# Masked attention scores kept in their PSUM bank, a later wait for the values, and a new split of the last head's blocks

## The reference

```python
x = x + tanh(g_xattn) * xattn(layernorm(x), ids, ctx, ctx, ctx)     # 4 experts: silu(h Wg) * (h Wu), then Wd
x = x + tanh(g_ffn)   * ffn(layernorm(x), ...)

# ffn, 16 heads of 32
q, k, v = rmsnorm(x) @ Wq.T, ... @ Wk.T, ... @ Wv.T
probs   = softmax(where(causal, q k^T / sqrt(32), min), -1)
attn    = (probs @ v) @ Wo.T
mod     = 0.1 * tanh(attn @ A)                                      # A: 512 x 16
h       = rmsnorm(residual, ln2)
gate    = silu(h @ W_in.T + mod * (h @ A) @ B)
out     = residual + (gate * (h @ W_up.T)) @ W_down.T               # hidden width 2048
```

## Time and profile before

| | us |
|---|---|
| median of 3 runs (lowest, highest) | 1045.88 (1045.06, 1047.07) |
| profiled execution, whole | 1046.06 |
| its span, first to last instruction | 1044.3 |
| PE / DVE / ACT / POOL busy | 1011.3 / 701.9 / 608.0 / 284.6 |

### The profile page before, as it was taken

The page is one execution under the profiler, slowest core; times in us unless marked ns, Lnnn a source line. Parts: engine busy times, 40 slices in busy tenths (PEclk is TensorE's granted clock), DMA queues, the critical chain, the costliest instruction groups (busy, mean ns, idle before and its releaser), DMA issues.

```text
span 1044.3 us, 16780 instructions
## 1 busy us (share of the span) xinstructions
PE 1011.3 (97%) x5140; PEld 831.4 (80%) x5141; DVE 701.9 (67%) x1837; ACT 608.0 (58%) x1447; POOL 284.6 (27%) x280
## 2 busy tenths in 40 slices
PE   6999999999999999999999999999999989999998
PEld 6787888777888887778888888778888877788887
DVE  7766755996665558985665479966655599854443
ACT  4464456997344448985444369963444489844432
POOL 4536124861000117650000148610001177400000
PEclk9999999999999999999999999999999999999999
DMA  6545133343222426443322354432334253322221
GB/s 236 195 151 171 40 121 96 77 119 132 94 90 90 131 62 169 97 133 115 104 91 91 111 157 92 117 122 91 92 102 147 64 149 92 91 81 90 90 90 51
DMA packets 47073, 115.78 MB, mean 111 GB/s; under 512 B 6800, under 2 KB 6800, under 8 KB 46096
## 3 DMA queue, kind: packets, MB, share of 16 engines
q1 hardware_dynamic: 43968, 105.06, 33.7%
q0 software_dynamic: 3040, 9.96, 2.8%
HBM read 76.46 MB, written 13.37 MB: 86 GB/s over the span
## 4 chain that ended last, share of the span: by engine, by line
PE 86%; DVE 11%; issue 1%; DMA 1%; POOL 1%; ACT 1%; SPq 0%; DVEq 0%; POOLq 0%
PE bank L534 68%; PE bank L731 7%; DVE big L1399 5%; PE bank L793 4%; DVE wr L1385 3%; PE bank L697 2%; PE bank L835 1%; PE bank L590 1%; PE bank L764 1%; PE bank L605 1%; PE bank L648 1%; DMA stack<-wr 0%; PE bank L570 0%; POOL wr L502 0%; DVE big L1422 0%
## 5 line engine op out<-in xcount | busy, mean ns | idle before, releaser
L534 PE MATMUL bank<-hT,wr 128*128 128x512 f32 x1488 | 358.2, 390 | 0.0
L534 PEld LDWEIGHTS bank<-hT,wr 128*128 128x128 f32 x1488 | 279.2, 188 | 60.8 <-issue 1.5
L534 PE MATMUL bank<-wr,actr 128*128 128x512 f32 (+1 forms) x1224 | 303.4, 397 | 2.2 <-DVE actr L1367 1.5
L534 PEld LDWEIGHTS bank<-wr,actr 128*128 128x128 f32 x1224 | 228.9, 190 | 50.8 <-issue 3.0
L490 POOL TENSOR_SCALAR big<-big,rr 128x256 f32<-128x256 f32 (+1 forms) x128 | 154.5, 1215 | 82.4 <-DVE rr L1405 82.4
L429 POOL TENSOR_TENSOR wqs<-wstage,wqs 128x512 fp32r<-128x512 f32 x32 | 43.1, 1358 | 433.6 <-ACT wqs L949 432.2
L1432 DVE SCALAR_TENSOR_TENSOR wr<-stream,lns,wr 128x256 fp32r<-128x256 f32 x256 | 121.7, 537 | 52.2 <-ACT wr L1059 52.2
L1033 ACT ACTIVATE big<-big,nb 128x512 f32<-128x512 f32 (+3 forms) x256 | 140.9, 557 | 11.5 <-DVE nb L1399 11.1
L1385 DVE TENSOR_TENSOR wr<-bank,wr 128x512 fp32r<-128x512 f32 (+1 forms) x224 | 126.0, 607 | 21.3 <-ACT wr L949 20.7
L949 ACT ACTIVATE wr<-bank 128x512 fp32r<-128x512 f32 (+1 forms) x224 | 110.1, 529 | 35.7 <-PE bank L534 20.2
L949 ACT ACTIVATE actr<-act_sb 128x512 fp32r<-128x512 f32 x64 | 40.4, 632 | 146.0 <-DVE act_sb L1446 146.0
(11 more groups left out here) (174 smaller groups left out, 988.0 us busy)
## 6 DMA issues: line engine op xcount, KB each, us to landing
stream<-in_wmlp SPq DMA_DIRECT2D x64, 512.0 KB, 4.0
stack<-wr SPq DMA_DIRECT2D x192, 128.0 KB, 2.3
stream<-in_wmlp SPq DMA_DIRECT2D x64, 256.0 KB, 2.7
big<-in_x SPq DMA_DIRECT2D x4, 1024.0 KB
big<-y_rows SPq DMA_DIRECT2D x4, 1024.0 KB, 5.8
residual<-big SPq DMA_DIRECT2D x4, 1024.0 KB
big<-residual SPq DMA_DIRECT2D x4, 1024.0 KB, 6.5
out<-big SPq DMA_DIRECT2D x3, 1024.0 KB, 4.8
```

Of the source, the lines that this page charges most:

```text
L534: mm = pe.matmul(dst, lhs(pl, k), rhs(pr, k), start=start and i == 0, stop=stop and i == n - 1, skip_group_check=skip)
```

## The change

- `maxima` writes the masked scores back into the bank that it reads (in place), no longer to `prob`. Its wait for `p_turned` is gone, and so is the wait for `res_out` ahead of the first head.
- `exponentials` reads the bank and writes `prob`. Blocks 2 and 0 share a bank, so the exponential of block 2 waits for the maxima of both.
- PE may write new scores into a bank only when the exponentials have read it: every such wait is now on `exp_ok` in place of `nb_ok`, with the same counts.
- The wait for `vst_lo` goes from ahead of the transposes to ahead of the first attend. The DVE copy to `vp` goes from `head_step` of head 0 to ahead of it.
- In the last head DVE scales blocks 3 and 2, POOL block 1 alone. The low-rank product runs whole (8 matmuls) in step 14; step 13 has no filling.

```diff
-NORM_DVE, NORM_ACT, NORM_POOL = 3, 0, (1, 2)
+NORM_DVE, NORM_ACT, NORM_POOL = (3,), 0, (1, 2)
+LAST_DVE, LAST_POOL = (3, 2), (1,)
...
 POOL normalise(n):
-                for qt in NORM_POOL:
+                for qt in NORM_POOL if n % H < H - 1 else LAST_POOL:
...
 PE scores_last(n, ...):
-                    pe.wait_ge(nb_ok, n * 4 - 3)
+                    pe.wait_ge(exp_ok, n * 4 - 3)
 PE scores_middle(n, ...):
-                    pe.wait_ge(nb_ok, n * 4 - 1)
+                    pe.wait_ge(exp_ok, n * 4 - 1)
 PE scores_second(n, ...):
-                    pe.wait_ge(nb_ok, n * 4)
+                    pe.wait_ge(exp_ok, n * 4)
...
 PE filling:
-                elif head >= LOW_RANK_FROM:
-                    low_rank_part(b, head - LOW_RANK_FROM)
+                elif head == LOW_RANK_AT:
+                    low_rank(b)
...
 PE head_step:
-                if j == 0:
-                    pe.wait_ge(vst_lo, b * NQ + q + 1)
                 if head < H - 1:
                     wait_probs(n + 1)
...
                 if head < H - 3:
-                    pe.wait_ge(nb_ok, (n + 3) * 4 - 1)
+                    pe.wait_ge(exp_ok, (n + 3) * 4 - 1)
...
+                    if j == 0:
+                        pe.wait_ge(vst_lo, b * NQ + q + 1)
                     attend(first, HI)
                     if head < H - 3:
-                        pe.wait_ge(nb_ok, (n + 3) * 4)
+                        pe.wait_ge(exp_ok, (n + 3) * 4)
...
 ACT exponentials(n, par):
-                for i, qt in enumerate((3, 2, 0, 1)):
-                    act.wait_ge(nb_ok, n * 4 + i + 1)
-                    rows = prob_rows(par, qt)
-                    a.activation(rows, rows, ACT.Exp, ...
+                for qt, maxima in ((3, 1), (2, 3), (0, 3), (1, 4)):
+                    act.wait_ge(nb_ok, n * 4 + maxima)
+                    bk, col, _ = SCORE[qt]
+                    a.activation(prob_rows(par, qt), bank[bk][:, col:col + P * (qt + 1)], ACT.Exp, ...
...
 DVE maxima(n, par):
-                if not first:
-                    dve.wait_ge(p_turned, (n - 1) * 3)
...
-                        v.tensor_tensor_reduce(prob_rows(par, qt), bank[bk][:, col:col + P * (qt + 1)],
+                        rows = bank[bk][:, col:col + P * (qt + 1)]
+                        v.tensor_tensor_reduce(rows, rows,
                                                masks[:, S - P * (qt + 1):S], -1.0, 3.0e38, ALU.add, ALU.min,
...
 DVE normalise(n, par):
-                rows = prob_rows(par, NORM_DVE)
-                v.tensor_scalar(rows, rows, rr[:, par, NORM_DVE:NORM_DVE + 1], None, ALU.mult).then_inc(pn_ok, 1)
+                for qt in NORM_DVE if n % H < H - 1 else LAST_DVE:
+                    rows = prob_rows(par, qt)
+                    ins = v.tensor_scalar(rows, rows, rr[:, par, qt:qt + 1], None, ALU.mult)
+                ins.then_inc(pn_ok, 1)
...
 DVE batch:
-                dve.wait_ge(res_out, (b + 1) * 16)
...
                 qk_low(b, 1, 1, SECOND_K)
+                dve.wait_ge(vp_done, b * 2 + 2)
+                v.tensor_copy(vp[:, 2:4, :, :].rearrange("p t h r -> p (t h r)"),
+                              bank[VALUES[1]][:, :]).then_inc(vpb_ok, 1)
```

More of the change, by code:

```diff
@@ L44 @@
 PACKED = 1280
-NORM_DVE, NORM_ACT, NORM_POOL = 3, 0, (1, 2)
+NORM_DVE, NORM_ACT, NORM_POOL = (3,), 0, (1, 2)
+LAST_DVE, LAST_POOL = (3, 2), (1,)
+POOL_ROWS = len(NORM_POOL) * (H - 1) + len(LAST_POOL)
 TURN_ORDER = (2, 1, 3, 0)
@@ L61 @@
 UP_PARTS, UP_FROM = 4, 9
-LOW_RANK_FROM = H - 3
+LOW_RANK_AT = H - 2
 PARTS = ((HI, HI), (LO, HI), (HI, LO))
@@ L745, in wait_probs @@
                 pe.wait_ge(pn_act, n + 1)
-                pe.wait_ge(pn_pool, (n + 1) * len(NORM_POOL))
+                last = n % H == H - 1
+                pe.wait_ge(pn_pool, n // H * POOL_ROWS + (POOL_ROWS if last else (n % H + 1) * len(NORM_POOL)))
             def stack_loads(b, head):
@@ L756, in project_part, with low_rank @@
                     project(b, q + 2, j // 2, half=j % 2)
[L758 to L762, removed]
+            def low_rank(b):
+                pe.wait_ge(exp_ok, (b + 1) * H * 4)
+                for k in range(DT):
                     for part in (HI, LO):
@@ L766, in low_rank_part @@
                                        skip_group_check=True)
-                if half == 1:
-                    mm.then_inc(ha_done, 1)
+                mm.then_inc(ha_done, 1)
             def filling(b, head):
@@ L907, in batch @@
                         head_step(b, q, j)
-                pe.wait_ge(nb_ok, (b + 1) * H * 4)
+                pe.wait_ge(exp_ok, (b + 1) * H * 4)
                 gate_product(0)
@@ L1028, in exponentials @@
             def exponentials(n, par):
-                for i, qt in enumerate((3, 2, 0, 1)):
-                    act.wait_ge(nb_ok, n * 4 + i + 1)
-                    rows = prob_rows(par, qt)
-                    a.activation(rows, rows, ACT.Exp, bias=nb[:, par, qt:qt + 1], scale=-1.0,
+                for qt, maxima in ((3, 1), (2, 3), (0, 3), (1, 4)):
+                    act.wait_ge(nb_ok, n * 4 + maxima)
+                    bk, col, _ = SCORE[qt]
+                    a.activation(prob_rows(par, qt), bank[bk][:, col:col + P * (qt + 1)], ACT.Exp, bias=nb[:, par, qt:qt + 1], scale=-1.0,
                                  accum_out=rs[:, par, qt:qt + 1]).then_inc(exp_ok, 1)
@@ L1389, in qk_low, with maxima @@
                 low(qk[:, q % 2, (Q_LO, K_LO)[which], :], bank[at][:, :], qk[:, q % 2, (Q_HI, K_HI)[which], :], qk_lo)
-            def maxima(n, par, first=False):
-                if not first:
-                    dve.wait_ge(p_turned, (n - 1) * 3)
+            def maxima(n, par):
                 for i, qts in enumerate(((3,), (2, 0), (1,))):
@@ L1419, in head_step @@
                     maxima(n + 2, j % 2)
[L1420 to L1423, removed]
                 for i, (bk, w, at) in enumerate(TURNED_BANKS):
@@ L1520, in batch @@
                 gate_up_low(b, 0, 0)
-                dve.wait_ge(res_out, (b + 1) * 16)
-                maxima(b * H, 0, first=True)
+                maxima(b * H, 0)
                 gate_up_low(b, 1, 1)
@@ L1525, in batch @@
                 qk_low(b, 1, 0)
-                maxima(b * H + 1, 1, first=True)
+                maxima(b * H + 1, 1)
                 qk_low(b, 1, 1, SECOND_K)
+                dve.wait_ge(vp_done, b * 2 + 2)
+                v.tensor_copy(vp[:, 2:4, :, :].rearrange("p t h r -> p (t h r)"),
+                              bank[VALUES[1]][:, :]).then_inc(vpb_ok, 1)
                 for q in range(NQ):
```

## The result

The changed kernel is **slower**: 1056.24 us (median of 4 runs, 1054.73 to 1057.19) against 1046.12 for the kernel before on the same chip (4 runs, 1045.06 to 1047.07). The ratio is 1.0085, 95% interval 1.0070 to 1.0100. By the medians the loss is 10.1 us and by the ratio 8.9. The profiled execution took 1054.73, its span is 1052.6, so profile against profile the loss is 8.7 us.

The account below looks back on a forecast made before the run. PE, busy 97% of the span, was taken as the bound. Per batch 2.28 - 1.1 - 0.4 + 0.5 = 1.28; four batches 5.1, less 1.5 once, +3.6 us: 1049.7 us, range 1043.5 to 1056.5.

Parts of the forecast that it names:

- part 1: PE's waits before writing scores into a bank, now for exponentials instead of maxima: +2.28 us a batch.
- POOL's full 1.0: Last head: POOL's scaling gets ahead of DVE's second one, low parts of head 14 come late, PE waits 1.0 a batch.
- its own signs: Forecast wrong if PE shows no idle time before block 3, or if maxima or head 15's second scaling grow.
- The ring of part 1: Steps 1 to 6: transposes, ACT copies, exponential, block 3, projection, next transposes; 4.56 or 4.90 us a turn, 28.38 against 26.10.
- The delay is eaten by the stall of head 0: Before the loop, PE's scores of head 2 wait for head 1's exponentials; PE's 2.10 us idle time absorbs this, costing nothing.
- Part 3: Head 0, values waited for later: POOL's queue is the next limit, so only -0.4 us a batch of 2.10 is kept.
- Part 2: Maxima in place without the wait for transposes: DVE period 3.78 instead of 4.02, heads 11 to 15, -1.1 us a batch.
- the 62 ns of the upper end: Highest extra time allowed for a DVE maximum writing to a bank, four writes a head, 0.25 us; 0 was taken.
- The rival that bank writes eat part 2: At 62 ns a write DVE's period is 4.03 and the in-place maxima gain nothing: 1054.1 us, chance 0.20.
- Reads by ACT, -33 ns: Exponentials of 512 columns reading a bank instead of SBUF shrink by about 33 ns; exponential to release 0.79 from 0.82.
- Part 4: Last head: new order gives nothing, but POOL may delay DVE's second scaling: +0.5 us a batch, between 0 and 1.0.
- The clock, -1.5 once: Second batch: TensorE's half clock over 3 us after the stall of head 0 goes away, -1.5 us once.

Follow-up runs that it names:

- The waits alone: Kernel before, with PE's waits on `nb_ok` turned into waits on `exp_ok` and nothing else: 1062.63 us, ratio 1.0138.
- the later weights: Changed kernel with POOL's weights of the third k projection made one step later: 1052.35 us, ratio 1.0047 to the kernel before.
- the last run above: Changed kernel with block 3 after the filling, weights one step later, head 1's maxima earlier, and the last-head edits undone: 1040.29 us, ratio 0.9927.
- block 3 late: Changed kernel with PE scoring block 3 of head m+3 behind the filling (projection) instead of ahead: 1044.96 us, ratio 0.9971 to the kernel before.
- the last head alone: Kernel before with only the last-head edits: DVE scales blocks 3 and 2, whole low-rank product in step 14; 1048.95 us, ratio 1.0013.
- the covered kernels: Changed kernel versions with block 3 scored behind the filling: 1044.96 us; with weights one step later 1042.07; with head 1's maxima also earlier 1039.49.
- part 3 alone: Kernel before with only the `vst_lo` wait moved to the first attend and the DVE copy ahead of the heads: 1041.59 us, again 1041.92.

## Why the prediction was right or wrong

The direction was right, the mechanism of part 1 too; the size was not: +3.6 us forecast, +10.1 measured by the medians (8.9 by the ratio, 8.7 by the profiles). That 1056.24 still lies within the stated range is luck: its upper end, 1056.5, stood for dear bank writes together with POOL's full 1.0 in the last head, and neither came to that. By its own signs the forecast was wrong in one point: the maxima did grow, by 0.10 us a head. In the third batch 1.53 us are missing: 0.88 ahead of the first transposes, 0.22 from there to head 2, 0.19 in the six steps, 0.24 behind them. They came by these steps:

- **The ring of part 1: right.** 28.38 forecast, 28.57 measured; legs of 2.34, 0.79 and 1.77 against 2.36, 0.93 and 1.69. The 0.93 includes the step from release to matmul that I had put in the last leg. Covering the wait by order gave 11.9 us back, 4 x 1.66 of it in the six steps and 4 x 1.05 in the step from head 1 to 2. What I left out is that the ring also turns in that step.
- **"The delay is eaten by the stall of head 0": wrong, and mis-sized by 0.88.** The waits alone show the delay paid whole and the stall still there. The working looked at PE alone. The stall's end was tied to the first transposes through maxima, DVE copy and POOL. In the changed kernel the copy is out of that chain, so the two edits together shorten the step to head 1 by 1.83. But the collision and the ring lengthen the next one by 1.65.
- **Part 3, -0.4: right alone, wrong here.** The same order of queues that I followed on POOL also decides what POOL and DVE do at one moment. I priced such a collision in the last head, where it did not happen, and not in head 2, where it did (0.93, by the later weights). It is the largest single loss, but the shorter step to head 1 hides most of it: the stretch as a whole misses the forecast by 0.22 only.
- **Part 2, -1.1: about half** (the last stretch's -0.36, less part 4's own +0.16, is -0.5; without part 4 and with the wait covered, in the last run above, it is 31.28 against 31.97, -0.7). Writing into the bank costs DVE, and neither my 0 nor the 62 ns of the upper end is right. Groups of the same shape, after (two rows) and before (one):

```profile
L1399 DVE CUSTOM_DVE_ANT_0 bank<-bank,masks 128x512 f32<-128x512 f32 x64 | 44.2, 691 | 2.9 <-PE bank L699 2.9
...
L1399 DVE CUSTOM_DVE_ANT_0 bank<-bank,masks 128x384 f32<-128x384 f32 x64 | 38.0, 593 | 2.2 <-PE bank L699 2.2
```
```profile
L1399 DVE CUSTOM_DVE_ANT_0 big<-bank,masks 128x384 f32<-128x384 f32 x64 | 35.4, 552 | 0.0
```

  The first maximum of a head keeps its time (691 against 688), the three behind it take 41 to 46 ns more, and from the first maximum to the low parts it is 1.75 us instead of 1.65. The period of DVE is therefore 3.89 (reciprocal at 678.97, the next at 682.86), not 3.78, against 4.02. The ring adds 0.26 in the step from head 10 to 11, but most of it comes back by head 14: with block 3 late the stretch is 31.47, only 0.13 shorter than the changed kernel's 31.60. The Trainium skill's page Perfetto Trace Analysis, section Optimizing Scalar/DVE Operations, was right in sign for DVE writes, with 65 ns a write more. It calls its figures engine-busy times, so the distance between starts is the nearer measure, and this trace has 0.10 us there for the four writes, some 25 ns each; the durations grow by 41 to 46 ns on three of four and by 3 on the first. The rival that bank writes eat part 2 gave 1054.1, next to the profile's 1054.73, but for another reason: they cost some 0.11 us a head, over five heads 0.5 a batch, where it had 1.1.
- **Reads by ACT, -33 ns: right for the first.** The exponentials of 512 columns take 694 ns against 728. But the accumulator read takes 209 against 192, so less than 20 ns of it remain on the way to the release.
- **Part 4, +0.5: did not happen.** In the last head DVE's two scalings ran back to back, the second of them while POOL's was under way:

```profile
686.75 0.17 DVE L1405 RECIPROCAL rr<-rs 128x4 f32<-128x4 f32 x1
...
686.96 1.04 DVE L1409 TENSOR_SCALAR big<-big,rr 128x512 f32<-128x512 f32 x2
687.01 1.23 POOL L492 TENSOR_SCALAR big<-big,rr 128x256 f32<-128x256 f32 x1 [1.44 <-DVE rr L1405]
687.36 0.64 DVE L1409 TENSOR_SCALAR big<-big,rr 128x384 f32<-128x384 f32 x1
```

  The part by itself costs 0.16 a batch in the rows, against the 0.5 forecast.
- **The clock, -1.5 once: the stretch is gone in this profile, but it was worth 1.0.** It was at 0.51 and is at 1.00. Before, it made the step behind the stall 1.5 longer, as forecast, but 0.6 of this was made up again in the six steps after it. Whether the low clock comes is not fixed by the kernel: the waits alone and the last head alone lost it in two and three batches, each time behind a wait of 1.6 to 2.1 us in head 0, while their other batches had the same wait and kept the clock.

What stays open: why the third to sixth steps of the covered kernels are still 4.5 to 4.8 long. One DVE scaling of 1.38 us beside POOL's work (head 4, at 634.57 with block 3 late) is part of it; the rest was not taken apart. Giving block 3 another bank wasn't tried.

## What to carry to other kernels

When a wait moves from one stage to the next, write down the whole ring of queues that it closes, and look for work of the same engine that can be put in front of the waiting instruction: here one swap was worth 12 us. Before a stall is counted on to hide a delay, ask what ends it, and whether the delayed work is upstream of that. A gain measured for one edit alone need not survive beside another: the order of two engines that disturb each other can turn on a few tenths of a us (0.08 behind or 0.34 ahead).

## What the runs showed of the hardware

- A DVE instruction that writes to the bank it reads takes 41 to 46 ns more than one that writes to SBUF if it is the second to fourth of a row (384, 128 and 256 columns), and 3 ns more if it is the first. The first is always the one of 512 columns, so place and width can't be told apart here. Its accumulator read goes from 83 to 141 ns. ACT saves 34, 21, 15 and 23 ns (512, 384, 256, 128 columns) by reading the bank.
- A DVE scaling of 512 columns that starts 0.08 behind a POOL instruction took 1.49 us instead of 0.49; one that started 0.34 ahead of it took 0.53. The Trainium skill's page SBUF — State Buffer, section Who interferes with whom, says that the first to issue holds the shared port, and these rows agree. The price can be read off: wherever POOL's TENSOR_TENSOR of the weights began 0.05 to 0.97 ahead of a scaling, the scaling ended 0.28 to 0.29 after POOL's instruction did. Leads of 0.05, 0.08, 0.19, 0.56 and 0.97 gave lengths of 1.52, 1.49, 1.38, 1.00 and 0.59 (before, after, before, and part 3 alone twice); the thirteen traces have 78 such rows. The 0.53 fits as well: it ends 0.28 after a POOL cast that had begun 0.35 ahead of it. For the last head I had drawn from the page that POOL, once waiting, goes ahead of DVE's second instruction; there it did not (1.04 us for two). The second, of 384 columns, began 0.35 behind POOL's scaling, took 0.64 and ended before it. Why this pair behaves otherwise than the weights is open.
- TensorE's half clock (0.51 of full, the 1.2 GHz level) followed a PE wait of 1.6 to 2.1 us in some batches and not in others of the same kernel, and made the step behind it 1.1 to 1.6 us longer each time. Over the whole attention of a batch 0.9 to 1.3 us of it remained (before, the waits alone, the last head alone).
